# The attention mask laid by eight 64-row, 32-column products instead of two full ones

## The reference

```
for i in range(6):
    x = attn_layer(shift_tokens(x), Wqkv[i], q_scale[i], k_scale[i], Wo[i]) + x
    x = ffn_layer(shift_tokens(x), ln_g[i], ln_b[i], W1[i], b1[i], W2[i], b2[i]) + x
```

```
mask = (it < jb) | (it > jb + w) | (jb == -1)
sim = jnp.einsum('bhwie,bhwje->bhwij', bq, bk2) * QK_SCALE
sim = jnp.where(mask, -jnp.finfo(sim.dtype).max, sim)
```

## Time and profile before

| | us |
|---|---|
| timed runs, median of 3 (lowest, highest) | 2013.35 (2007.73, 2013.68) |
| span of the profiled execution | 2010.7 |
| PE busy, PEld busy | 1805.9, 1311.9 |
| DVE busy | 1557.0 |
| POOL busy | 1455.2 |
| ACT busy | 1164.3 |
| first step of the layers to the last, roughly | 200 to 1990 |

### The profile page before, as it was taken

One profiled execution on the slowest core, in us unless ns is written; L12 is line 12 of the kernel. 1 busy time (PEld: TensorE's weight loads), 2 busy tenths in 40 slices (PEclk: granted clock), 3 DMA queues, 4 the chain that ended last, 5 costly groups with the idle time before them and its releaser, 6 DMA issues. The chain is left out here.

```text
span 2010.7 us, 85596 instructions
## 1 busy us (share of the span) xinstructions
PE 1805.9 (90%) x34280; PEld 1311.9 (65%) x34280; DVE 1557.0 (77%) x2776; ACT 1164.3 (58%) x1966; POOL 1455.2 (72%) x967
## 2 busy tenths in 40 slices
PE   7774689999999999999999999999999999999995
PEld 3453466676776666766666666667676667676764
DVE  4764688887888878888788788887887888878864
ACT  2311356666666666666666666666666666666662
POOL 3221688877887778777877787778777877787771
PEclk9875899999999999999999999999999999999997
DMA  4000122223222223222223322233222232222220
GB/s 151 2 3 1 44 65 65 59 54 86 73 70 53 55 63 91 59 70 63 61 53 84 77 68 55 52 82 81 63 58 59 63 86 63 70 63 55 55 58 22
DMA packets 93581, 123.43 MB, mean 61 GB/s; under 512 B 27760, under 2 KB 41808, under 8 KB 93392
## 3 DMA queue, kind: packets, MB, share of 16 engines
q1 hardware_dynamic: 93232, 122.42, 24.2%
q10 hardware_dynamic: 288, 0.13, 0.0%
HBM read 20.74 MB, written 1.05 MB: 11 GB/s over the span
## 5 line engine op out<-in xcount | busy, mean ns | idle before, releaser
L999 POOL TENSOR_TENSOR across<-unit,turns 128x1024 f32<-128x1024 f32 x192 | 497.4, 2591 | 279.7 <-issue 268.4
L1006 POOL TENSOR_TENSOR rotated<-along,across 128x1024 f32<-128x1024 f32 x192 | 496.7, 2587 | 14.2
L1151 DVE TENSOR_REDUCE sums<-squares 128x16 f32<-128x1024 f32 x192 | 234.2, 1220 | 173.2 <-ACT squares L1054 173.1
L1247 PE MATMUL turn<-identity,rotated 128*128 128x128 f32 x1536 | 205.2, 277 | 36.4 <-POOL rotated L1006 36.4
L1247 PEld LDWEIGHTS turn<-identity,rotated 128*128 128x128 f32 x1536 | 172.6, 141 | 98.9 <-issue 83.4
L1032 POOL TENSOR_TENSOR along<-unit,turns 128x1024 f32<-128x1024 f32 x96 | 228.3, 2378 | 0.0
L1352 PE MATMUL proj_a<-w_qkv,shift_a 128*128 128x512 f32 x384 | 189.9, 617 | 36.4 <-DVE unit L1176 30.1
L1113 ACT COPY val<-proj_a 128x1024 f32<-128x1024 f32 x96 | 97.2, 1013 | 181.3 <-PE proj_a L1352 181.3
L1377 PEld LDWEIGHTS att<-o_t,w_o 128*128 128x128 f32 x1536 | 188.0, 193 | 6.1 <-issue 1.0
L1377 PE MATMUL att<-o_t,w_o 128*128 128x128 f32 x1536 | 188.3, 276 | 0.0
L1280 PE MATMUL proj_a<-w_qkv,shift_a 128*128 128x512 f32 x384 | 183.5, 601 | 4.3 <-POOL shift_a L988 3.0
(11 more groups left out here) (203 smaller groups left out, 3445.2 us busy)
## 6 DMA issues: line engine op xcount, KB each, us to landing
v_win<-val SPq DMA_DIRECT2D x1536, 64.0 KB, 2.0
w_qkv<-wqkv_dram SPq DMA_DIRECT2D x18, 512.0 KB, 3.8
w_o<-wo_dram SPq DMA_DIRECT2D x6, 512.0 KB, 4.6
where<-positions_dram SPq DMA_DIRECT2D x1, 2048.0 KB, 11.4
w_ffn<-ffn_dram SPq DMA_DIRECT2D x12, 170.5 KB, 2.3
w_ffn<-ffn_dram SPq DMA_DIRECT2D x6, 192.0 KB, 2.3
x_tok<-x_dram SPq DMA_DIRECT2D x4, 256.0 KB, 4.3
out_dram<-final SPq DMA_DIRECT2D x4, 256.0 KB, 2.4
```

What stands on the lines that cost most here:

```text
L999: pool.tensor_tensor(a[:, :, ::-1, :], u, table, ALU.mult).then_inc(acrossed[j], 1)
L1006: pool.tensor_tensor(rotated[j][:, :, :], along[j][:, :, :], across[j][:, :, :], ALU.add).then_inc(rotated_in[j], 1)
L1151: dve.tensor_reduce(sums[:, j, :], squares[j][:, :, :], AX.X, ALU.add).then_inc(summed[j], 1)
L1247: mm = pe.transpose(bank[:, TILE * (i % 4):TILE * (i % 4) + TILE], buffer[:, TILE * i:TILE * i + TILE], identity[:, :])
```

## The change

PE lays the mask with eight bfloat16 products, one for each window and head par, each of 64 rows and 32 columns of weights and 512 moving columns, into the same place as the scores of that window and head. The band repeats every 32 rows, so the first 32 rows of each half serve all windows. Three of the four windows always take the band of other tiles; window 0 takes it from a small buffer `band_now`. ACT fills that buffer with one copy of 128 x 64 bfloat16 per step, for the tile to come, right behind the carry of the keys (L1108), and once ahead of the first step. PE waits for `k_laid`, then for `band_chosen`, with a lone increment behind them. The choice of the band in the loop moves from PE's registers to ACT's. In `band_masks` the first version now hides the window before in all rows, since only window 0 reads it.

```diff
+        band_now = sb("band_now", [128, 2 * WINDOW], BF16)
+        band_chosen = sem("band_chosen")
+        FIRST_OF_LAYER, OTHER = 0, 1
...
             @block.scalar
             def _(act):
+                act.copy(band_now[:, :], band_bf[:, FIRST_OF_LAYER, :]).then_inc(band_chosen, 1)
...
                         act.activation(k_t[:, :, 0:WINDOW], k_t[:, :, TILE:TILE + WINDOW], ACT.Copy,
                                        scale=carry_scale[:, 0:1]).then_inc(k_carried, 1)
+                        following = a + 1
+                        which = (FIRST_OF_LAYER if following % TILES == 0 else OTHER) if isinstance(a, int) \
+                            else (tile_of(following) + 15) // 16
+                        act.copy(band_now[:, :], band_bf[:, which, :]).then_inc(band_chosen, 1)
...
                     if live["a"]:
-                        which = (mask_first if a % TILES == 0 else mask_other) if isinstance(a, int) \
-                            else (tile_of(a) + 15) // 16
-                        band = band_bf[:, which, :].unsqueeze(1).broadcast_to([128, PAIRS, 2 * WINDOW])
                         pe.wait_ge(k_laid, 2 * a + 2)
-                        for par in range(2):
-                            pe.matmul(bank_t[:, par, :].rearrange("p (a c) -> p a c", a=PAIRS), identity_bf[:, :], band,
-                                      start=True, stop=False, skip_group_check=True)
+                        pe.wait_ge(band_chosen, a + 1)
+                        stand_alone(pe, passed)
+                        for w in range(BLOCKS):
+                            for par in range(2):
+                                rows = slice(HEAD * par, HEAD * par + HEAD)
+                                band = (band_now[rows, :] if w == 0 else band_bf[rows, OTHER, :]).unsqueeze(1)\
+                                    .broadcast_to([HEAD, PAIRS, 2 * WINDOW])
+                                pe.matmul(bank_t[WINDOW * w:WINDOW * w + WINDOW, par, :].rearrange("p (a c) -> p a c", a=PAIRS),
+                                          identity_bf[rows, HEAD * par:HEAD * par + WINDOW], band,
+                                          start=True, stop=False, skip_group_check=True)
...
-    first = hidden | ((a < WINDOW) & (c < WINDOW))
+    first = hidden | (c < WINDOW)
```

More of the change, by code:

```diff
@@ L1242, in _ @@
                 pe.wait_ge(centre_made, 2)
-                mask_first, mask_other = 0, 1
                 def transposes(bank, buffer, j, signal):
```

## The result

The changed kernel takes 2016.62 us (median of 15 runs, 2011.19 to 2020.99); the kernel before, on the same chip, 2010.53 us (2004.88 to 2015.08). The ratio is 1.003, 95% interval 1.0018 to 1.0042: slower, by about 6 us. The profiled execution took 2014.24 us with a span of 2012.4; the span before was 2010.7.

A forecast was written before the change was run, and what follows sets the result against it. The prediction took the value product's wait for DVE's unite to bound each step, so PE's mask saving would mostly become waiting. Span 2010.7 less 0 to 1.5 us, plus 2.65 carried over, gave 2012.6, stated as 2012.5; range 2001 to 2022.

The forecast's parts named there:

- scatter around no change: Whole kernel: nothing moves, 2012.5 us, chance 0.70; this case's own range is 2006 to 2019 us.
- wider rivals beyond: Whole kernel: gain shows (0.14), two products at once (0.10), one by one (0.02), ACT or the wait costs (0.04).
- What bounds the loop: Loop steps: value product waits for DVE's unite; that cycle sets the step, with 30.1 us of such waits in all.
- the other branch: PE between mixing and value product: mask and scores have 0.25 us to spare in even steps, about 0.45 in odd.
- The mask's occupancy: PE, mask's first start to scores' first: 0.31 to 0.41 us instead of 0.53, 11 to 21 us over 96 steps.
- The 0.10 us turn from full to small products: PE, changing from 128-row products to the scores' 64-row, 32-column ones: 0.10 us stays and moves ahead of the mask.
- The rival of two products at once: Mask on PE: one product per row half at once, 0.94 us; even steps lose 0.16, 2021 us; chance 0.10.
- The copy on ACT and PE's second wait: ACT behind the carry: 0.4 us with registers, hidden in 1.89 us idle; PE's wait 0 to 0.1 us, taken as 0.
- Sum: Whole kernel: span 2010.7 less 0 to 1.5 us, 2010.0 in the middle; with 2.65 us carried over, 2012.6.
- the steps without a wait for DVE: The 7 steps where the value product doesn't wait for DVE's unite: saving counts there, 1.5 us at most.
- whether the granted clock falls inside the layers: PE inside the layers: busy share goes from 94 to about 93 of 100 us, no fall from 1.00 expected.

The follow-up runs named there:

- e7: Changed kernel with the scale-spreading product (even steps) and three output-product pairs (odd steps) moved ahead of the value product, DVE's and ACT's work too: 1977.6 us, 0.9831 of before.
- e8: Kernel before, full mask products kept, with the scale-spreading product (even steps) and two output-product pairs (odd steps) moved ahead of the value product: 1986.7 us, ratio 0.9878.
- e2: Kernel before, its two full mask products kept, with ACT's copy of the band and PE's wait and lone increment added: 2011.8 us, ratio 1.0004.
- e3: Changed kernel with two full mask products in the written-out steps, the eight small ones only in the loop: 2008.9 us, 0.9996 of the kernel before.
- e1: Changed kernel without ACT's band copy and PE's wait for it, all eight products reading the band of other tiles: 2018.1 us, 1.0026 of the kernel before.
- e4: Changed kernel with the eight small mask products only in the written-out steps, two full ones in the loop: 2013.7 us, 1.0016 of the kernel before.
- e5: Kernel before with each full mask product cut into four full-array products of 128 columns: 2012.7 us, ratio 1.0007.
- e6: Kernel before with 128 lone semaphore increments on PE ahead of the layers: 2028.1 us, ratio 1.0080.
- e9: Kernel before with 128 lone semaphore increments at the very start of PE's program: 2033.3 us, ratio 1.0106.
- e10: Changed kernel with 128 lone semaphore increments at the very start of PE's program: 2028.9 us, 1.0091 of the kernel before.
- e11: Changed kernel with 64 lone semaphore increments at the very start of PE's program: 2015.1 us, 1.0031 of the kernel before.
- e12: Changed kernel with work moved ahead of the value product, and two full mask products in the written-out steps: 1973.6 us, 0.9821 of the kernel before.

## Why the prediction was wrong

The forecast was no change, 2012.5 us; the time came out within the range, but slower beyond the interval. That the range holds it is luck: it allowed some 6 us of scatter around no change and wider rivals beyond, and no term of it stood for what made the kernel slower.

- **What bounds the loop: right.** The value product waits for DVE's unite, mask and scores are on the other branch. Shown by the round that stayed at 36.5 us while the wait grew, and by e7 and e8, where most of the work moved off the cycle came out of the time.
- **The mask's occupancy: right in kind, off in size.** 0.31 to 0.41 us predicted, 0.22 to 0.23 measured. The 0.10 us turn from full to small products doesn't move ahead of the mask: the heads' transposes, started at 1024.93, are followed by the mask at 1025.95, 1.02 us later, where two groups of transposes in a row are 0.98 apart (1023.95 to 1024.93). The saving is 0.30 us a step (0.52 - 0.22), and 96 x 0.30 = 29 us is near the 28 us by which the wait rose; the prediction had 11 to 21.
- **The rival of two products at once did not occur.** By the sentence of the Trainium skill on row groups ("TensorE: Matmul & The Clock Gate", section "Part 3: Packing small matmuls — row/col tiling") two would run at once; the prediction worked that out as 0.84 us, 0.94 with the turn. The trace doesn't agree: eight products of 512 columns, four of them in each row half, held PE for 0.22 us, about the time of one.
- **The copy on ACT and PE's second wait: right.** 0.228 us for the copy and 0.147 for the register piece, in 1.96 us of idle time behind them; e2 shows no cost that can be told.
- **The step that failed: "Sum".** It laid one price on all 96 steps, that of a round in the middle of the trace, and gave the steps without a wait for DVE a gain of 0 to 1.5 us. The eight steps ahead of the loop, its first round and the steps behind it are another case: their instructions come over the DMA while they run. The change puts 16 instructions in place of 4 there (weight loads counted) and takes 0.3 us out of the same run of work. In place of a gain of up to 1.5 us stands a loss near 6, which goes when the small products leave these steps (e3). The gaps, each at a block's limit, are what the profile shows of it there. The sum also had no term for the clock outside the loop (next point). Had I looked for idle time marked "issue" inside a burst, I would have found the 0.18 us gap at 348.42 in the trace of before, and with it a term that the sum lacked.
- **The clock outside the loop, which the prediction left out.** It asked only whether the granted clock falls inside the layers. Outside the loop it moves between 0.5 and 1.0 of the full one (the levels of 1.2 and 2.4 GHz), and this moves the time by microseconds. The last output product of the program shows it (PE's row), with busy times and granted clock of the stretch around it in the changed kernel and in e3 (the clock is the number ahead of the last two); changed kernel, before, e3:

```profile
1972.81 3.62 PE L1389 MATMUL att<-o_t,w_o 128*128 128x128 f32 x16
...
1967.00:1977.00 10.00, 7.82 (x55) 6.92 (x55) 2.00 (x4) 1.77 (x3) 0.18 (x1) 0.50 0.01 2
```
```profile
1971.23 3.36 PE L1377 MATMUL att<-o_t,w_o 128*128 128x128 f32 x16
```
```profile
1966.04 1.95 PE L1395 MATMUL att<-o_t,w_o 128*128 128x128 f32 x16
...
1963.00:1973.00 10.00, 7.09 (x42) 5.95 (x43) 2.59 (x7) 5.63 (x9) 0.79 (x2) 1.00 0.01 2
```

  From its start to the next piece it holds PE for 3.41, 3.20 and 1.79 us. The granted clock is 0.50 from 1967 to 1977 us in the changed kernel, where it follows the gap of 2.49 us, and 1.00 from 1963 to 1973 in e3. All seven kernels with a gap behind the loop (changed, e1, e4, e5, e6, e7, e9) have this product at 3.25 to 3.41 us and take 70.8 to 73.5 us from the last value product to the end. Of the seven without, five have 1.78 or 1.79 and take 65.3 to 67.5 (e3, e8, e10, e11, e12), two have 3.20 and take 69.2 and 70.7 (e2 and before). The means are 72.6 and 67.5 us: beside a gap of 2.1 to 2.8 us stand 5 us of time. The balance above has only 1.29 us there because the kernel before ran at the lower clock in its profile without a gap. That the gap brings the lower clock is argued from seven of seven against two of seven, not tested.
- **A gap and the order of DVE and POOL.** Between the tenth and the eleventh value product the changed kernel lost 1.02 us with no gap in that step. DVE's multiplication of the keys ran beside POOL's addition; in the changed kernel, then in e1:

```profile
374.90 2.35 POOL L1009 TENSOR_TENSOR rotated<-along,across 128x1024 f32<-128x1024 f32 x1
375.02 3.31 DVE L1243 TENSOR_TENSOR along<-unit,turns 128x1024 f32<-128x1024 f32 x1
...
381.25 1.96 PE L1303 MATMUL proj_b<-w_qkv,shift_a 128*128 128x512 f32 x4 [1.23 <-DVE hidden L1201]
```
```profile
374.99 1.22 DVE L1237 TENSOR_TENSOR along<-unit,turns 128x1024 f32<-128x1024 f32 x1
375.14 3.29 POOL L1009 TENSOR_TENSOR rotated<-along,across 128x1024 f32<-128x1024 f32 x1
```

  In these two cases the one that starts first takes its normal time (POOL 2.35 us, DVE 1.22) and the other is longer by 0.9 to 2.1 us. The 0.68 us gap just ahead in the changed kernel, where e1 has 0.35, comes before this turn of the order; that it caused it is argued, not shown.

What stays open: how the loss divides between the number of instructions, their density and their place. With full mask products in the written-out steps the gaps sum to 0 to 4.0 us in eight kernels (before, e2, e3, e5, e6, e8, e9, e12), with small ones to 3.7 to 6.8 in six (changed, e1, e4, e7, e10, e11). The small ones have more, but at one placement (e9 against e10) the times are in the other order. And a profile's sum of gaps doesn't give the time by itself: e1 and the changed kernel have nearly the same gaps and 217.13 and 220.63 us from the first to the 13th value product. Of these 3.5 us, 2.5 fall between the first and the third value product, where the granted clock is 0.86 in e1 and 0.79 in the changed kernel, and 1.0 us between the tenth and the eleventh. Open too is what share of the 6 us comes from the gaps themselves and what from the clock behind them.

## What to carry to other kernels

Before you price an edit by the loop's steady step, ask which branch sets that step, and whether the steps outside the loop are the same case: code that runs once has to be fetched while it runs, and a dense run of small products can outpace that. Spare time on the busiest engine is worth nothing until work is moved from the cycle into it; then the changed kernel gained 35 us and the kernel before 26, with one pair of the output product less moved. And a difference of 0.3% between two long programs can be where their code happens to lie, and at which clock its ends happen to run: shift both, and compare the clock outside the loop, before you credit the edit.

## What the runs showed of the hardware that was not expected

- Eight bfloat16 products of 64 rows, 32 columns and 512 moving columns, with distinct row halves and column quarters, start within 0.024 us and hold PE together for 0.22 us, about as long as one full product (0.21).
- PE's instructions come in packets of 16 KB, 46 in this program; a loop of two steps, 1348 matmuls and weight loads a round in the changed kernel, fetches nothing from its second round on.
- A break in that supply lasts 0.2 to 2.8 us (the longest in e7, at 1929.14 us), stands at a multiple of 256 instructions from the next, and ends 1.2 to 1.6 us after a packet has landed (35 of 35).
- 128 lone semaphore increments at the start of PE's program put its first product off by 16 us (4.54 to 20.49); they start 0.153 us apart, where each lasts 0.051.
